# Grouped expert layer: gating moved to GpSimd, last product in three passes of split operands

## The reference, cut to what matters

```python
h = silu(einsum('ecd,edm->ecm', xb, w1)) * einsum('ecd,edm->ecm', xb, w3)   # 64 wide per expert
yb = einsum('ecm,emd->ecd', h, w2)
y = yb[expert, position] * w        # w is the token's gate for that expert; summed over its 8 experts
```

## Time and profile before

| | us |
|---|---|
| median of 3 runs | 3358.24 (3357.71 to 3359.0) |
| the profiled execution, its own time | 3355.26 |
| its span in the trace | 3353.5 |
| PE busy | 2531.6 (75% of the span) |
| DVE busy | 2400.1 (72%) |
| POOL busy | 1326.5 (40%) |
| ACT busy | 1309.0 (39%) |
| first product of `m0x` starts | 1345.95 |
| last addition to `H` in `m0x` ends | 1644.2 |

### The profile page before, as it was taken

How to read it: one execution, slowest core, us unless ns; L and a number is a source line. 1 busy time by engine, 2 the same in 40 slices (tenths; PEclk the granted TensorE clock), 3 DMA queues, 4 the chain that set the end, 5 groups by cost and what they waited for, 6 DMA issues and landing times. The chain is left out here.

```text
span 3353.5 us, 29110 instructions
## 1 busy us (share of the span) xinstructions
PE 2531.6 (75%) x8891; PEld 1513.4 (45%) x8891; DVE 2400.1 (72%) x3486; ACT 1309.0 (39%) x1993; POOL 1326.5 (40%) x792
## 2 busy tenths in 40 slices
PE   0677868766786872999757979489998679868599
PEld 0223323322232331666534737367776457623366
DVE  4599799759979987455546475658888558759556
ACT  0544344344435431222253343247775347520222
POOL 1189669717975981111123416110000310014256
PEclk9889879877997985999878989779999879979799
DMA  4054144205514420556300000021210021000021
GB/s 130 8 126 114 32 99 114 57 8 116 109 43 94 109 70 11 136 134 142 72 20 7 20 6 0 4 78 70 76 57 28 4 71 70 17 11 14 10 80 63
DMA packets 86713, 203.71 MB, mean 61 GB/s; under 512 B 12832, under 2 KB 25200, under 8 KB 78032
## 3 DMA queue, kind: packets, MB, share of 16 engines
q1 hardware_dynamic: 86064, 201.02, 23.5%
q0 software_dynamic: 512, 1.05, 0.1%
HBM read 199.15 MB, written 2.88 MB: 60 GB/s over the span
## 5 line engine op out<-in xcount | busy, mean ns | idle before, releaser
L529 DVE TENSOR_TENSOR m1x_HS<-m1x_R,m1x_HS 128x512 fp32r<-128x512 f32 x256 | 175.8, 692 | 69.1 <-ACT m1x_HS L497 64.7
L490 ACT ACTIVATE m1x_R<-m1x_ph,m1s_W 128x512 f32<-128x512 f32 x256 | 176.4, 689 | 107.0 <-PE m1x_ph L305 106.3
L1295 POOL TENSOR_TENSOR t2x_KM<-t2x_KT,t2x_HM 128x2048 f32<-128x2048 f32 x8 | 28.8, 3604 | 430.8 <-ACT t2x_KT L1368 415.2
L1635 POOL TENSOR_TENSOR t3xs_QH<-t3xs_HS,t3xa_Q 128x1536 f32<-128x1536 f32 x16 | 62.1, 3880 | 346.4 <-DVE t3xs_HS L1621 346.4
L826 DVE TENSOR_TENSOR m0x_T<-m0x_S,m0x_pb 128x512 f32<-128x512 f32 x128 | 88.1, 689 | 131.0 <-PE m0x_pb L305 130.8
L1987 PE MATMUL t0x1fs_acc<-t0x1fs_HC,g_ident 128*128 128x512 f32 x256 | 134.5, 658 | 37.9 <-POOL t0x1fs_HC L2068 37.8
L1987 PE MATMUL t0x0fs_acc<-t0x0fs_HC,g_ident 128*128 128x512 f32 x256 | 133.2, 651 | 38.1 <-POOL t0x0fs_HC L2068 38.0
L812 ACT ACTIVATE m0x_S<-m0x_pa 128x512 f32<-128x512 f32 x128 | 76.5, 598 | 214.0 <-PE m0x_pa L305 214.0
L1987 PE MATMUL t0x1bs_acc<-t0x1bs_HC,g_ident 128*128 128x512 f32 x256 | 132.9, 651 | 35.5 <-POOL t0x1bs_HC L2068 35.3
L1987 PE MATMUL t0x0bs_acc<-t0x0bs_HC,g_ident 128*128 128x512 f32 x256 | 132.9, 651 | 35.3 <-POOL t0x0bs_HC L2068 35.2
L2068 POOL TENSOR_TENSOR t0x0bs_HC<-t0x0bs_HS,t0x0bs_CB 128x1024 f32<-128x1024 f32 x64 | 150.2, 2409 | 8.5 <-DMA t0x0bs_CB<-t0x0b_bc_rows 3.8
(11 more groups left out here) (889 smaller groups left out, 7543.5 us busy)
## 6 DMA issues: line engine op xcount, KB each, us to landing
m0x_GS<-m_gate_rows SPq DMA_DIRECT2D x64, 512.0 KB, 6.5
t0x0fs_CB<-t0x0f_bc_rows SPq DMA_DIRECT2D x32, 512.0 KB, 6.3
t0x0bs_CB<-t0x0b_bc_rows SPq DMA_DIRECT2D x32, 512.0 KB, 6.5
t0x1fs_CB<-t0x1f_bc_rows SPq DMA_DIRECT2D x32, 512.0 KB, 6.4
t0x1bs_CB<-t0x1b_bc_rows SPq DMA_DIRECT2D x32, 512.0 KB, 6.8
m1x_GS<-m_gate_rows SPq DMA_DIRECT2D x16, 1024.0 KB, 4.7
m1s_W<-in_L_w SPq DMA_DIRECT2D x16, 514.0 KB, 3.3
m2x_GS<-m_gate_rows SPq DMA_DIRECT2D x8, 1024.0 KB, 4.6
```

Source lines behind the costliest of these rows:

```text
L490: a.activation(R[:, s % 4, :], ph[s % 4][:, :], ACT.Relu, bias=W[:, e % RAW, weights.cut + c:weights.cut + c + 1]).then_inc(relu_ready, 1)
L529: v.tensor_tensor(HS[:, s % 4, 1, :], R[:, s % 4, :], HS[:, s % 4, 0, :].bitcast(F32), ALU.subtract).then_inc(low_made, 1)
L1295: nc.gpsimd.tensor_tensor(KM[:, i % 2, :, :], keys, spread(HM[:, :], W), ALU.mult).then_inc(km_made, 1)
L1635: nc.gpsimd.tensor_tensor(QH[:, j % 2, 0:SPLIT], HS[:, j % 2, 0:SPLIT], Q[:, 0:SPLIT], ALU.mult).then_inc(qh_pool, 1)
```

## The change

POOL takes over the gating: it multiplies `S` by `GS` into `SG` (L783 of the changed kernel), one instruction of 128x512 a step, before DVE's first multiplication. `bend` on DVE then makes `HF` = `SG` * `pb` (L848). ACT makes the high part of `HF` into `HR` (L834, a copy to float32r), two steps behind its silu, and DVE makes the low part, `HF` minus the high part (L852, `low`), in the place in its order where `gate` stood. `second` on PE becomes a three-pass `product` of the split w2 and `HR`, three steps behind `first` instead of two. `Weights` splits all 384 columns of a unit instead of 256. POOL's splits, which stood by themselves in its program, now stand between the gates, behind the gate of a unit's second group. first(s) now waits for `S` of step s - 2 before `pa`, and for `HF` of step s - 2 (semaphore `hidden`) before `pb`. `HR` has four buffers, `SG` and `HF` two.

```diff
@@ def grouped_experts
-    W, WR = weights.W, weights.WR
+    WR = weights.WR
+    LAG = 3
...
             def _(pool):
-                for u in range(RAW, UNITS):
-                    pool.wait_ge(w_loaded[u % RAW], 16 * (u // RAW + 1))
-                    weights.split(nc.gpsimd, u % RAW, u, None)
+                for s in range(STEPS):
+                    u, g = place(s)
+                    if g == 0:
+                        pool.wait_ge(g_loaded[u % GB], 32 * (u // GB + 1))
+                    pool.wait_ge(s_ready, s + 1)
+                    if s >= 2:
+                        pool.wait_ge(hidden, s - 1)
+                    nc.gpsimd.tensor_tensor(SG[:, s % 2, :], S[:, s % 2, :], GS[:, u % GB, tokens(g)], ALU.mult).then_inc(gated, 1)
+                    if g == 1 and RAW <= u + 1 < UNITS:
+                        pool.wait_ge(w_loaded[(u + 1) % RAW], 16 * ((u + 1) // RAW + 1))
+                        weights.split(nc.gpsimd, (u + 1) % RAW, u + 1, None)
...
                     if s >= 2:
-                        pe.wait_ge(t_ready, s - 1)
+                        pe.wait_ge(s_ready, s - 1)
...
+                    if s >= 2:
+                        pe.wait_ge(hidden, s - 1)
                     product(pe, pb[s % 2][:, :], [WR[:, j, n, P:2 * P] for n in range(2)], x).then_inc(b_ready, 1)
...
-                    pe.wait_ge(gated, s + 1)
-                    pe.matmul(acc[g][:, :], W[:, u % RAW, 2 * P:3 * P], HF[:, s % 3, :], start=(u == 0),
-                              stop=(u == UNITS - 1), skip_group_check=True).then_inc(summed, 1)
...
+                    pe.wait_ge(low_ready, s + 1)
+                    product(pe, acc[g][:, :], [WR[:, u % RAW, n, 2 * P:3 * P] for n in range(2)],
+                            [HR[:, s % 4, n, :] for n in range(2)], u == 0, u == UNITS - 1).then_inc(summed, 1)
...
             def _(act):
...
+                for s in range(STEPS + 2):
+                    if s < STEPS:
+                        act.wait_ge(a_ready, s + 1)
+                        if s >= 2:
+                            act.wait_ge(gated, s - 1)
+                        nc.scalar.activation(S[:, s % 2, :], pa[s % 2][:, :], ACT.Silu).then_inc(s_ready, 1)
                     if s >= 2:
...
+                        n = s - 2
+                        act.wait_ge(hidden, n + 1)
+                        if n >= 4:
+                            act.wait_ge(summed, n - 3)
+                        nc.scalar.activation(HR[:, n % 4, 0, :], HF[:, n % 2, :], ACT.Copy).then_inc(high_ready, 1)
...
                 def bend(s):
-                    dve.wait_ge(s_ready, s + 1)
+                    dve.wait_ge(gated, s + 1)
                     dve.wait_ge(b_ready, s + 1)
                     if s >= 2:
...
+                        dve.wait_ge(low_ready, s - 1)
+                    v.tensor_tensor(HF[:, s % 2, :], SG[:, s % 2, :], pb[s % 2][:, :], ALU.mult).then_inc(hidden, 1)
+
+                def low(s):
+                    dve.wait_ge(high_ready, s + 1)
+                    v.tensor_tensor(HR[:, s % 4, 1, :], HF[:, s % 2, :], HR[:, s % 4, 0, :].bitcast(F32),
+                                    ALU.subtract).then_inc(low_ready, 1)
...
-            weights = Weights(nc, s, ins["L0_units"], 4, 2 * P, 0)
+            weights = Weights(nc, s, ins["L0_units"], 4, 3 * P, 0)
```

More of the change, by code:

```diff
@@ L732, in grouped_experts @@
         S = st.sb("S", [P, 2, GROUP])
-        T2 = st.sb("T2", [P, 2, GROUP])
-        HF = st.sb("HF", [P, 3, GROUP])
+        SG = st.sb("SG", [P, 2, GROUP])
+        HF = st.sb("HF", [P, 2, GROUP])
+        HR = st.sb("HR", [P, 4, 2, GROUP], F32R)
         OT = st.sb("OT", [P, T])
@@ L742, in grouped_experts @@
         s_ready = st.sem("s_ready")
-        t_ready = st.sem("t_ready")
         gated = st.sem("gated")
+        hidden = st.sem("hidden")
+        high_ready = st.sem("high_ready")
+        low_ready = st.sem("low_ready")
         summed = st.sem("summed")
@@ L789, in second @@
                     u, g = place(s)
-                    pe.wait_ge(gated, s + 1)
-                    pe.matmul(acc[g][:, :], W[:, u % RAW, 2 * P:3 * P], HF[:, s % 3, :], start=(u == 0),
-                              stop=(u == UNITS - 1), skip_group_check=True).then_inc(summed, 1)
-                for s in range(STEPS + 2):
+                    pe.wait_ge(low_ready, s + 1)
+                    product(pe, acc[g][:, :], [WR[:, u % RAW, n, 2 * P:3 * P] for n in range(2)],
+                            [HR[:, s % 4, n, :] for n in range(2)], u == 0, u == UNITS - 1).then_inc(summed, 1)
+                for s in range(STEPS + LAG):
                     if s < STEPS:
                         first(s)
-                    if s >= 2:
-                        second(s - 2)
+                    if s >= LAG:
+                        second(s - LAG)
                 for g in range(GROUPS):
@@ L807, in _ @@
             def _(act):
-                for s in range(STEPS):
-                    act.wait_ge(a_ready, s + 1)
-                    if s >= 2:
-                        act.wait_ge(t_ready, s - 1)
-                    nc.scalar.activation(S[:, s % 2, :], pa[s % 2][:, :], ACT.Silu).then_inc(s_ready, 1)
+                for s in range(STEPS + 2):
[4 more added lines that the diff above has]
+                        nc.scalar.activation(S[:, s % 2, :], pa[s % 2][:, :], ACT.Silu).then_inc(s_ready, 1)
+                    if s >= 2:
+                        n = s - 2
[3 more added lines that the diff above has]
+                        nc.scalar.activation(HR[:, n % 4, 0, :], HF[:, n % 2, :], ACT.Copy).then_inc(high_ready, 1)
                 for g in range(GROUPS):
@@ L840, in _ @@
                     if s:
-                        gate(s - 1)
+                        low(s - 1)
                 for g in range(GROUPS):
```

## The result

The changed kernel takes 3454.49 us (median, 3447.41 to 3456.77) against 3358.22 us of the kernel before: a ratio of 1.0283, 95% interval 1.0265 to 1.0301. It is 96 us slower, where 21 us were forecast and 3418 us was the upper end of the range. The profiled execution took 3456.77 us, its span is 3455.0 us; the last addition to `H` in `m0x` ends at 1740.4 us in it, 96 us later than before.

The account below looks back on a forecast made before the run. PE's work was taken to bound the kernel before, a loop of waits the changed one: +19.9 split units, -3.0 other steps, +2.0 start, +1.7 end, +0.5 routing, sum +21 us on 3358.2, so 3379 us; range 3350 to 3418.

Parts of the forecast that it names:

- the sentence on SP: SP's gate loads have two units of slack and its weight loads more than a step to land: no cost.
- The clock: PE's pauses in the stage, 1.5 us a unit, don't lower its granted clock of 1.00: no cost.
- The port and the order: POOL and DVE's `low` exclude each other at SBUF; with the written order, waits set the unit: +19.9 us over 28 units.
- The loop of 9.68 us: From POOL's third-group gate to the same gate a unit later: 9.68 us, against 8.97 us a unit before.
- splits of 1.4 us: Sign of being right: POOL's weight splits, 1.01 us each when alone, take 1.4 us.
- Rival 1: DVE doesn't wait for a running POOL multiplication, so `low` slips in: -16 us, 3342 us; chance 0.20.
- rival 3: In the splits only POOL or only DVE is held off: 9.0 to 9.3 us a unit, 3360 us; chance 0.08.
- Rival 2: When a gate ends, POOL's next gate goes before a waiting `low`: 10.96 us a unit, 3415 us; chance 0.10.
- rival 4: ACT's copy reloads the activation table each turn: over 3500 us; chance 0.02.
- The three passes: On PE, the last product in three passes takes 0.68 us instead of 0.86 us.
- the routing term: In the routing stage, POOL's first eight splits grow and meet more DVE instructions: +0.5 us, between 0 and 1.1.
- a port always in use: Limiting case where the POOL and DVE port never idles: 8.4 us a unit, -16 us in all.

Follow-up runs that it names:

- the gates early: Changed kernel with SP's weight loads moved behind the next unit's gate loads, so gates are requested one unit earlier: 3379.79 us, ratio 1.0064.
- without the dispute: Changed kernel with gates requested earlier, `low` reading PSUM and POOL's splits apart: 3340.95 us; "in it" is the same with `low` reading SBUF twice: 3358.59 us.
- both edits: Changed kernel with gates requested one unit earlier and `low` reading PSUM (product made in place in `pb`): 3362.55 us, 9.04 us a unit.

## Why the prediction was wrong

**The step that failed** is the sentence on SP: "three buffers and so two units of slack; ... nothing for both". It priced how long buffers are free, not when SP reaches the request. SP works its program in order, and before the request for unit u + 1 stands the wait for all of unit u - 1. Once the wait was said to come "a step later", what is queued behind it had to be named: the gates. The kernel before shows how little room there was (timeline of SP and DVE):

```profile
1499.77 1.08 SPq L763 DMA_DIRECT2D m0x_GS<-m_gate_rows  x2
```
```profile
1508.19 0.69 DVE L835 TENSOR_TENSOR m0x_HF<-m0x_T,m0x_GS 128x512 f32<-128x512 f32 x1
```

DVE, which gated a step only behind its product of the step after, first used those gates 8.42 us after the request, and they need 7.4 us or more (the loop above): 1 us of room. The change takes from both sides. `second` trails by three steps, so the request goes out a step later, and the gate stands right behind the silu instead of at the step's end. Between the request and that gate PE now has only first(4u + 3), `second` of one step and the `pa` of the new unit to do: 1.37 + 0.68 + 0.68 us, and 0.80 us of silu, 3.5 us at the prediction's prices. The gates are wanted 4.9 us sooner after their request than before, and come 7.4 - 3.5 = 3.9 us too late; in the unit above the silu ended at 1497.81 and the gate began at 1501.71, 3.9 us later. (The 4.4 us of the waits also hold the time in which the silu wasn't done.) Walked as the prediction walked its own loop, SP's is 7.4 + 1.34 + 0.75 + 0.74 + 0.74 + 0.4 = 11.4 us, longer than 9.68 us and so the bound: some 3427 us by the prediction's sum. Measured were 12.2 us, and two more prices are seen in the rows of the unit above: the port (`second` waits for an L852 of 1.14 us, 0.3 us) and the clock (`second` takes 1.15 instead of 0.68 us).

**The clock** was priced at nothing, from a stretch in which PE pauses often; a clock under 1.00 stood among the signs of being wrong, and it came. In the predicted loop, whose pauses are 0.6 us and less, the price is right: 1.00 with the gates early. In the changed kernel it is wrong, and it is part of the 2.7 us a unit that the queue costs. Two units in which the clock stayed at 1.00, columns as in the earlier trace rows:

```profile
1518.50:1530.25 11.75, 9.32 (x37) 6.45 (x37) 6.09 (x9) 4.62 (x8) 7.76 (x7) 1.00 0.44 106
1530.25:1541.95 11.70, 9.33 (x37) 6.45 (x36) 6.07 (x9) 4.60 (x8) 7.75 (x7) 1.00 0.44 106
```

They take 11.7 us, which is the walk of 11.4 us and the port's 0.3 us, so the clock's share of the mean of 12.2 us is an estimated 0.5 us.

**The port and the order** were right in mechanism and size. The loop of 9.68 us, from the scans and splits of the earlier trace rows alone, came out at 9.6 us, and the 3379 us at 3379.79 us, as soon as SP's wait was out of it. The walk is in that trace, point by point and within about 0.1 us: from the first of three gates (of the third group) over `second`, the silu, the second group's gate and the two splits to 1514.39, where the next such gate begins, 9.59 us after the first.

```profile
1504.80 4.21 POOL L783 TENSOR_TENSOR m0x_SG<-m0x_S,m0x_GS 128x512 f32<-128x512 f32 x3
...
1507.91 0.50 PE L303 MATMUL m0x_acc<-m0x_HR,m0s_WR 128*128 128x512 f32 x1
...
1509.61 0.60 ACT L828 ACTIVATE m0x_S<-m0x_pa 128x512 f32<-128x512 f32 x1 [2.14 <-PE m0x_pa L305]
...
1510.29 1.29 POOL L783 TENSOR_TENSOR m0x_SG<-m0x_S,m0x_GS 128x512 f32<-128x512 f32 x1 [1.28 <-ACT m0x_S L828]
...
1511.54 1.46 POOL L329 TENSOR_TENSOR m0s_WR<-m0s_W,m0s_ZERO 128x384 fp32r<-128x384 f32 x1
...
1513.08 1.35 POOL L333 TENSOR_TENSOR m0s_WR<-m0s_W,m0s_WR 128x384 fp32r<-128x384 f32 x1
```

That the two times agree to 1 us is luck, since the loop came out 2 us smaller over the stage and the kernel before stood 3 us higher beside this run than beside the first. L852 meets gates (1074 ns there, 972 in the changed kernel); splits of 1.4 us were 1.46 and 1.34. Rival 1, no hold-off, and rival 3, only one side held, are refuted: without the dispute `low` takes 684 ns and a gate 1290 ns, in it 986 and 1501 ns. Rival 2, POOL first, too: in the run with the gates early three gates back to back take 4.21 us, 0.37 us over three times 1.28, since a `low` that waits goes in between them. The table was loaded once, so rival 4 falls as well.

**The small terms.** The three passes cost what was said. The start of `m0x` came 2.2 us later than before, not 0.5, but with its spread of 13 us over the traces the routing term is not settled. One sum is a little off: a port always in use, 8.4 us a unit, makes -14 to -15 us with the other terms, not -16; nothing hangs on it. Some 5 of the 101.5 us by which the profiled span grew lie behind the stage, where nothing was changed; no run explains them.

## What to carry to other kernels

Price a queue by where a request stands in its program, not by how many buffers are free: write down for each load what its issuer waits for ahead of it, when the data is first used, and the landing, and walk that as a loop like any other. A change that uses a loaded operand earlier in the step, or lets the end of the step trail further, takes room from loads that it doesn't touch. And where a helper engine is put between two stages of a pipeline, spread its other work over the gaps, and let the instructions beside it read PSUM where they can.

## What was not expected of the hardware

PE's clock fell after some of its pauses and not after others, and the length of the pause doesn't tell which. Busy time and clock of the changed kernel around the pause of 2.31 us:

```profile
1498.00:1502.00 4.00, 3.44 (x15) 2.48 (x14) 1.12 (x2) 1.45 (x3) 0.29 (x1) 1.00 0.50 113
1502.00:1504.00 2.00, 0.25 (x1) 0.25 (x2) 0.99 (x2) 0.87 (x2) 2.00 (x2) 1.00 0.00 0
1504.00:1507.00 3.00, 2.91 (x9) 2.00 (x9) 2.04 (x3) 0.36 (x1) 2.92 (x4) 0.70 0.00 0
1507.00:1510.00 3.00, 3.00 (x12) 2.35 (x11) 1.69 (x2) 1.12 (x2) 2.52 (x3) 0.73 0.95 227
```

PE falls to the lower level (1.2 GHz) only after it has resumed and is busy again: its passes take 0.43 us from 1505.53 on, and 0.23 us again from 1508.80 on. Two other pauses of the same kernel, each with the 5 us behind it:

```profile
1441.87 0.50 PE L303 MATMUL m0x_pb<-m0s_XR,m0s_WR 128*128 128x512 f32 x1 [1.62 <-DVE m0x_HF L848]
1441.87:1446.87 5.00, 4.91 (x14) 3.65 (x15) 2.73 (x4) 1.73 (x3) 4.92 (x5) 0.69 0.41 107
```
```profile
1454.78 0.50 PE L303 MATMUL m0x_pb<-m0s_XR,m0s_WR 128*128 128x512 f32 x1 [2.48 <-DVE m0x_HF L848]
1454.78:1459.78 5.00, 4.64 (x18) 3.22 (x18) 2.71 (x4) 1.95 (x4) 4.92 (x5) 1.00 0.42 111
```

After 1.62 us it fell, after 2.48 us it didn't, and the stretch of the earlier trace rows has a pause of 2.50 us at 1.00. With pauses of 0.6 us once a unit (both edits) the clock was 1.00 throughout. What decides it is not shown by these runs. What is shown is that a pause can be paid for twice, and that here the slow passes stood in the very loop that made the pause.
